# A four-stage sequence kernel on one core: expert affinities by exp and a reciprocal with the choice over three steps, and the last stage's norm placed behind its routing

## What is computed

```python
def _layernorm(x, axis=-1, eps=1e-05):
    m = jnp.mean(x, axis=axis, keepdims=True)
    v = jnp.var(x, axis=axis, keepdims=True)
    return (x - m) / jnp.sqrt(v + eps)

# first layer's experts: 32 experts, the 8 largest affinities of each token, one shared expert
logits = jnp.dot(x.astype(jnp.float32), Wr) + br
aff = jax.nn.sigmoid(logits)
top_v, top_i = jax.lax.top_k(aff, K)
top_w = top_v / (jnp.sum(top_v, axis=-1, keepdims=True) + 1e-09)
w_full = w_full.at[jnp.arange(T)[:, None], top_i].set(top_w)
gate = silu(jnp.einsum('th,ehi->eti', x, Wg) + bg[:, None, :])
up = jnp.einsum('th,ehi->eti', x, Wu) + bu[:, None, :]
down = jnp.einsum('eti,eih->eth', gate * up, Wd) + bd[:, None, :]
routed = jnp.einsum('te,eth->th', w_full, down)

# second layer's experts: 8 heads of 32 features, 16 experts, the 2 largest of a softmax
w = jax.nn.softmax(t @ expert_emb, axis=-1)
topw, topi = jax.lax.top_k(w, K)
hmid = jax.nn.gelu(jnp.einsum('td,edi->tei', t, W1) + b1, approximate=False)
eo = jnp.einsum('tei,eio->teo', hmid, W2) + b2

x = _layernorm(x + _L0_attn_ref(x, ...))
x = _layernorm(x + _L0_ffn_ref(x, ...))
x = _layernorm(x + _L1_attn_ref(x, ...))
x = _layernorm(x + _L1_ffn_ref(x, ...))
```

## Time and profile before

| | us |
|---|---|
| median of 3 runs | 3381.89 |
| lowest and highest | 3381.45, 3384.49 |
| profiled execution, device time | 3384.75 |
| its span | 3382.9 |
| mean granted TensorE clock | 0.96 of full |

### The profile page before, as it was taken

One profiled execution on the slowest core, in us unless ns is written; L12 is line 12 of the kernel. 1 busy time (PEld: TensorE's weight loads), 2 busy tenths in 40 slices (PEclk: granted clock), 3 DMA queues, 4 the chain that ended last, 5 costly groups with the idle time before them and its releaser, 6 DMA issues. The chain is left out here.

```text
span 3382.9 us, 39560 instructions
## 1 busy us (share of the span) xinstructions
PE 3024.1 (89%) x11504; PEld 1714.0 (51%) x11504; DVE 2661.7 (79%) x3528; ACT 2297.8 (68%) x3491; POOL 2350.0 (69%) x1680
## 2 busy tenths in 40 slices
PE   3589999999999999998889999998977789999997
PEld 1157676667666667776334443443432344444442
DVE  5989999999999997554799999999997445555543
ACT  2467676767767676664676677677653688888886
...
GB/s 96 13 88 135 126 134 125 123 132 125 128 129 125 131 123 131 146 147 102 60 69 69 72 71 67 75 69 72 70 72 66 64 99 99 105 105 105 105 105 90
DMA packets 199619, 335.40 MB, mean 99 GB/s; under 512 B 21379, under 2 KB 57380, under 8 KB 199020
## 3 DMA queue, kind: packets, MB, share of 16 engines
...
## 5 line engine op out<-in xcount | busy, mean ns | idle before, releaser
L1452 POOL TENSOR_TENSOR c_hc<-c_h,c_c_rep 128x1024 f32<-128x1024 f32 x256 | 603.6, 2362 | 198.3 <-DVE c_h L1503 142.6
L1503 DVE TENSOR_TENSOR_SCAN c_h<-c_decay,c_carry,c_v_ps 128x512 f32<-128x512 f32 x512 | 632.0, 1273 | 0.0
L1987 POOL TENSOR_TENSOR d_acc<-d_acc,d_prod 128x512 f32<-128x512 f32 x240 | 312.2, 1310 | 449.0 <-DVE d_prod L2055 448.5
L1945 ACT ACTIVATE d_hmid<-d_up,d_b 128x1024 f32<-128x1024 f32 x512 | 532.4, 1117 | 82.0 <-PE d_up L1840 81.9
L1351 ACT ACTIVATE c_decay<-c_dt,c_a_cols 128x512 f32<-128x512 f32 x512 | 359.5, 719 | 301.4 <-DVE c_h L1503 288.6
L1197 PE MATMUL c_y_ps<-c_hc,ident 128*128 128x512 f32 x1024 | 504.9, 617 | 65.4 <-POOL c_hc L1452 56.4
L716 POOL TENSOR_TENSOR ab_inner_low<-ab_inner,ab_inner_high 128x512 fp32r<-128x512 f32 x264 | 341.5, 1294 | 211.2 <-ACT ab_inner_high L583 209.2
L572 ACT ACTIVATE ab_gate_ps<-ab_gate_ps,ab_raw_d 128x512 f32<-128x512 f32 x264 | 174.4, 661 | 416.1 <-PE ab_gate_ps L417 414.7
L2055 DVE SCALAR_TENSOR_TENSOR d_prod<-d_ring,d_b,d_w_rep 128x512 f32<-128x512 f32 x240 | 180.2, 751 | 267.2 <-PE d_ring L1850 151.7
L698 POOL TENSOR_TENSOR ab_hc<-ab_h,ab_c_rep 128x512 f32<-128x512 f32 x256 | 331.2, 1294 | 72.5 <-DVE ab_h L779 67.1
L704 POOL TENSOR_TENSOR ab_gu_low<-ab_raw_gu,ab_gu_high 128x512 fp32r<-128x512 f32 x264 | 341.5, 1294 | 4.4 <-ACT ab_gu_high L559 4.4
...
## 6 DMA issues: line engine op xcount, KB each, us to landing
...
c_c_rep<-c_c_scratch SPq DMA_DIRECT2D x256, 256.0 KB, 3.1
d_w_rep<-d_w_scratch SPq DMA_DIRECT2D x256, 256.0 KB
...
```

The source lines that it names most:

```text
L1452: nc.gpsimd.tensor_tensor(hc[:, q % HC], h[:, q % HR], c_rep[:, q % BC].unsqueeze(1).broadcast_to([P, PAIR, CH]), ALU.mult).then_inc(hc_re ...
L1503: nc.vector.tensor_tensor_scan(out=h[:, q % HR, m, :], data0=decay[:, i % DEC, :], data1=v_ps[m][:], initial=carry[:, i:i + 1], op0=ALU.mu ...
L1945: nc.scalar.activation(hmid[:, (2 * q + r) % HM], up_ps[(2 * q + r + c * 2 * NU) % UP][:], ACT.Gelu, bias=b1[:, e:e + 1]).then_inc(gelu_re ...
L1987: nc.gpsimd.tensor_tensor(acc[:, s, g, :], acc[:, s, g, :], prod[:, q % PR, :], ALU.add).then_inc(add_ready, 1)
```

## The change

Two independent edits. In `layer0` the affinities are now `exp(-x)` on ScalarE, and VectorE adds 1 and takes the reciprocal (`affinity`, two instructions over 128 x 128); the choice of the eight, until now two steps, is spread over three: `affinity` and `pick` at step 16, `drop_top` at 17, `share` at 18. The way back moves with it by one step: `Q_BACK` 19, `Q_WEIGHTS` 20, `Q_STORE` 21. In `layer1_experts` four slots move: mean and `centre` from pair 11 to 14, `scale` from q = 20 to 25, the square from behind q = 25 to behind q = 31.

```diff
--- before.py
+++ after.py
@@ -124,7 +124,7 @@
     STEPS = E1
 
     Q_RES1, Q_MEAN_A, Q_CENTRE_A, Q_SQUARE_A, Q_VAR_A, Q_DEV_A, Q_SCALE_A = 3, 5, 6, 7, 8, 9, 11
-    Q_LOGITS, Q_KEEP, Q_TURN, Q_AFF, Q_PICK, Q_BACK, Q_WEIGHTS, Q_STORE = 12, 13, 14, 15, 16, 18, 19, 20
+    Q_LOGITS, Q_KEEP, Q_TURN, Q_AFF, Q_PICK, Q_BACK, Q_WEIGHTS, Q_STORE = 12, 13, 14, 15, 16, 19, 20, 21
     Q_PROJ, Q_SPREAD = (16, 20, 22), (17, 21, 23)
     Q_RES0, Q_LOAD_X = 19, (12, 26)
     Q_RES_B, Q_MEAN_B, Q_CENTRE_B, Q_SQUARE_B, Q_VAR_B, Q_LOG, Q_SCALE_B = OFF + 1, OFF + 3, OFF + 4, OFF + 5, OFF + 6, OFF + 7, OFF + 8
@@ -238,7 +238,7 @@
 
         LOADS = 10 * 16
         CONSTS = 4
-        ROUTE = 3 * BPC + 5
+        ROUTE = 3 * BPC + 8
 
         def is_int(c, *values):
             return isinstance(c, int) and c in values
@@ -627,7 +627,7 @@
                         if not is_int(i, 1):
                             act.wait_ge(route, (i - 1) * ROUTE)
                         nc.scalar.activation(aff[:], work_ps[:, 0:BPC * NE].rearrange("p (b e) -> p b e", b=BPC),
-                                             ACT.Sigmoid).then_inc(work_left, 1)
+                                             ACT.Exp, scale=-1.0).then_inc(work_left, 1)
                     if n == Q_WEIGHTS and has(i, "back"):
                         act.wait_ge(work_ready, item(i, "back") + 1)
                         if not is_int(i, 1):
@@ -823,26 +823,37 @@
                     nc.vector.tensor_tensor(xT[:, half, cols(c)], zc[:, half], work_ps[:], ALU.mult
                                             ).then_inc(done, 1)
 
-            def pick(i):
+            def affinity(i):
                 c = i - 1
                 dve.wait_ge(work_left, item(i, "turn") + 1)
                 dve.sem_inc(route, 1)
+                nc.vector.tensor_scalar(aff[:], aff[:], 1.0, None, ALU.add).then_inc(route, 1)
+                dve.wait_ge(route, c * ROUTE + 2)
+                nc.vector.reciprocal(aff[:], aff[:]).then_inc(route, 1)
+
+            def pick(i):
+                c = i - 1
+                dve.wait_ge(route, c * ROUTE + 3)
+                dve.sem_inc(route, 1)
                 for b in range(BPC):
                     nc.vector.max(top[:, b, :], aff[:, b, :]).then_inc(route, 1)
-                dve.wait_ge(route, c * ROUTE + BPC + 1)
+                dve.wait_ge(route, c * ROUTE + BPC + 4)
                 nc.vector.reduce_sum(total[:], top[:], axis=AX_X).then_inc(route, 1)
+
+            def drop_top(i):
+                c = i - 1
                 for b in range(BPC):
                     nc.vector.match_replace(out=rest[:, b, :], in_to_replace=top[:, b, :], in_values=aff[:, b, :],
                                             imm_value=0.0).then_inc(route, 1)
-                dve.wait_ge(route, c * ROUTE + BPC + 2)
+                dve.wait_ge(route, c * ROUTE + BPC + 5)
                 nc.vector.tensor_scalar(total[:], total[:], 1e-9, None, ALU.add).then_inc(route, 1)
-                dve.wait_ge(route, c * ROUTE + 2 * BPC + 3)
+                dve.wait_ge(route, c * ROUTE + 2 * BPC + 6)
                 nc.vector.reciprocal(total[:], total[:]).then_inc(route, 1)
 
             def share(i):
                 c = i - 1
                 nc.vector.tensor_tensor(rest[:], aff[:], rest[:], ALU.subtract).then_inc(route, 1)
-                dve.wait_ge(route, c * ROUTE + 2 * BPC + 5)
+                dve.wait_ge(route, c * ROUTE + 2 * BPC + 8)
                 for b in range(BPC):
                     nc.vector.tensor_scalar(w_c[:, b, 0:NE], rest[:, b, :], total[:, b:b + 1], None, ALU.mult
                                             ).then_inc(route, 1)
@@ -870,10 +881,14 @@
                         scale(i - 1, xa_done)
                         dve.wait_ge(xa_done, i * 2)
                         dve.sem_inc(work_left, 1)
-                    if n == Q_PICK and has(i, "turn"):
-                        pick(i)
-                    if n == Q_PICK + 1 and has(i, "turn"):
-                        share(i)
+                    if has(i, "turn"):
+                        if n == Q_PICK:
+                            affinity(i)
+                            pick(i)
+                        if n == Q_PICK + 1:
+                            drop_top(i)
+                        if n == Q_PICK + 2:
+                            share(i)
                     if n == Q_RES0 and below(i, NCH):
                         if not is_int(i, 0):
                             dve.wait_ge(work_ready, item(i, "var_a") + 1)
@@ -1621,8 +1636,8 @@
 
 
     U_HALF, U_HEAD = (1, 2), (2, 3, 4, 4, 5, 6, 6, 7)
-    U_LOGITS, U_TURN, U_VAR, U_OUT, U_MEAN, U_BACK = 8, 9, 9, 10, 11, 13
-    Q_SCALE, Q_EXP, Q_PICK, Q_SQUARE = 20, 19, 20, 25
+    U_LOGITS, U_TURN, U_VAR, U_OUT, U_MEAN, U_BACK = 8, 9, 9, 10, 14, 13
+    Q_SCALE, Q_EXP, Q_PICK, Q_SQUARE = 25, 19, 20, 31
 
     def small(c, u):
```

## The result

| | before | after |
|---|---|---|
| median, us | 3381.67 (4 runs) | 3429.89 (4 runs) |
| lowest and highest | 3378.96, 3384.49 | 3425.15, 3432.97 |
| span of the profiled execution | 3382.9 | 3431.2 |
| mean granted TensorE clock | 0.96 | 0.95 |

The ratio is 1.014, 95% interval 1.0127 to 1.0152. The change costs 48.2 us where the prediction said 10.0: the side was right, the size was not.

A forecast was written before the change was run, and what follows sets the result against it. It took TensorE and VectorE, both near full, to bound layer0, and broadcast loads the last stage. Iterations 2 to 6 gave 5 x (0.77 + 0.80) = 7.9 us, iteration 1 +1.3, iteration 7 +0.8: +10.0, 3391.9 us, range 3384.0 to 3398.5.

The forecast's parts named there:

- Part 2: VectorE, layer0: addition 0.82 us and reciprocal 0.95 us, with waits 1.85 us; net +0.77 us at the gate of step 20.
- Part 1: ScalarE without the sigmoid's table loads: VectorE's 1.08 us wait at step 16 ends in each of iterations 2 to 7.
- where they stand does not matter: The choice's remaining instructions, in three steps instead of two, cost nothing wherever they stand from step 16 to step 20's gate.
- Part 3: TensorE's projection at step 20 waits 0.80 us for ScalarE's later copies out of the shared bank, iterations 2 to 6.
- Part 4: The moved slots in the last stage are hidden by the stream of weight loads; value 0.
- upper end of the range: 3398.5 us: VectorE's net at step 20's gate +1.53 us in place of +0.77, plus part of a costlier last stage.
- "no stall" rival: The projection at step 20 does not wait, as ScalarE runs further ahead of TensorE; +5.9 us, 3387.8; chance 0.17.

The follow-up runs named there:

- e4: The changed kernel with the addition of 1 on ScalarE instead of VectorE; 3423.34 us, ratio 1.0123.
- e11: The changed kernel with GpSimd's L704 over 256 in place of 512 columns in every step, VectorE's program unchanged; 3415.14 us, ratio 1.0097.
- e1: The changed kernel with the sigmoid and its table loads back, without addition and reciprocal, choice still in three steps; 3419.39 us, ratio 1.011.
- e14: The changed kernel with GpSimd's L691 two steps later, at step 21 in place of 19; 3409.67 us, ratio 1.0082.
- e12: The changed kernel with TensorE given products of zeros: 12 ending step 17, 10 ahead of the turning of the weights, 9 behind it; 3447.86 us, ratio 1.0195.
- e7: The changed kernel with the addition and the four products of share on ScalarE instead of VectorE; 3388.19 us, ratio 1.0019.
- e3: The kernel before with the last stage's four moved slots alone; 3380.60 us, ratio 0.9995.

## Why the prediction was wrong in size

**Part 2, the addition: the step that failed first.** It took 0.82 us, 0.28 and a wait of 0.54 read from L844, with the longest L844, 1.12, as its upper end. It took 2.69 on average, and from step 16 to the gate of step 20 iteration 3 lost 5.4 us where the prediction had 0.77. The waits of L844 before were, in iterations 2 to 7, those of an instruction that met GpSimd just ahead of a pause (in iteration 3 GpSimd's L698 ended at 528.15 and its next instruction began at 529.72); the mistake was to take a wait met at one place as its bound at another. What sets it is GpSimd's row of instructions at that very step; in iterations 2 to 7 it lasts to the first idle time in that row. Part 1 took away ScalarE's two table loads; the sums stopped there and never asked what GpSimd would then be doing when VectorE arrived. The prediction weighed a rule of the Trainium skill, page "SBUF — State Buffer", section "Who interferes with whom": an instruction of VectorE in a two-port mode or with two inputs in SBUF is shut out for the whole of a GpSimd instruction that started first, one with a single input in SBUF and outside those modes is not. For the reciprocal the traces agree, but not by the eight equal lengths in after, of which six fell in a pause of GpSimd: it is e4 that shows it (0.94 us inside L707) and e11 (0.95 inside L698). For the products the rule's length fits, one GpSimd instruction at a time. For the addition it falls short: L830 sat through three GpSimd instructions in iterations 2 to 6, and through six in iteration 7 (6.02 us), though only through one in iteration 8.

**Part 2, "where they stand does not matter": the larger error.** The same instructions moved from step 17 to 18 took 27.0 us in all in place of 6.7. e1 shows the split alone (+37 us) and e14 how much of it is L691's neighbourhood (20 us). That was open to sight: GpSimd's 2.4 us instruction stood at step 19 in the trace of before (534.18). Iteration 1, where the prediction took GpSimd for mostly quiet and forecast +1.3, lost 4.1, with the four products at 3.7 us in place of 1.6.

**The clock was not in the sum at all.** In iteration 3 the clock was at its lower level behind waits of 3.24 and 2.73 us; before, its longest wait in steps 16 to 20 was 1.62 us and the clock stayed. At step 21 that cost 4.5 us in all (e12).

**Part 1 was right**: no table load ahead of L629, and -1.13 to -1.17 us at step 16 in iterations 2 to 7 where 1.08 was forecast.

**Part 3 was right and mostly unseen.** The wait of the projection is 0.70 us where 0.80 was forecast, in e7, e12 and e14 in each of iterations 2 to 6. In after it shows as 0.44 and 0.73 in iterations 4 and 6 and is missing in the others: TensorE came late anyway. It moves step 21 by 0.43, not by the whole wait.

**Part 4 was right**: 0 (e3, and the streams).

In busy time from the grouped rows the terms are: addition 21.5, products 27.0 - 6.7 = 20.3, reciprocal 7.6, subtraction and small addition 3.5 - 6.2 + 2.0 - 3.4 = -4.1, tables 6 x -1.16 = -7.0, clock 4.5, copies 5 x 0.43 = 2.2: 45.0. That it comes so near to 48.2 is partly luck, as a busy time isn't yet a delay and the steps at 18 and 23 are left out; the sizes of its large terms are measured. The starts of L794 give the delay itself: +4.1 us in iteration 1, +36.0 in 2 to 6, +6.7 in 7 and +0.9 in 8, 47.7 together, where the prediction had 1.3, 7.9, 0.8 and 0. The rival closest to it was the upper end of the range: 1.53 in place of 0.77, still a wait of one GpSimd instruction. No rival had the addition held for a chain, or the products held at all. With the addition and the products off VectorE (e7) the change costs 6.4 us, under the forecast's 10.0. That this is near the "no stall" rival's 5.9 speaks not for that rival, as the projection does wait in e7.
